# Gate and up projections of a gated feed-forward layer: seven block products in place of eight, with the weight factors kept in DRAM

## What is computed

```python
def ffn(x, w_gate, w_up, w_down):
    h = silu(x @ w_gate) * (x @ w_up)
    h_sparse = _sparsify_2to4(h)      # of each 4 neighbours the 2 with the largest |h|
    return h_sparse @ w_down
x = x + tanh(g_xattn[0]) * cross_attention(layernorm(x), ctx, mask)
x = x + tanh(g_ffn[0]) * ffn(layernorm(x), w_gate, w_up, w_down)
```

## Time and profile before

| | |
|---|---|
| median of 3 runs | 1212.21 us (1211.08 to 1212.95) |
| the profiled execution, from first to last instruction (span) | 1210.4 us |
| PE busy | 1189.7 us, 98% |
| DVE busy | 755.0 us, 62% |
| ACT busy | 428.7 us, 35% |
| POOL busy | 103.4 us, 9% |
| DMA | 80.48 MB, 66 GB/s over the span; 235 to 320 GB/s in the attention phase |

### The profile page before, as it was taken

The page is one execution under the profiler, slowest core; times in us unless marked ns, Lnnn a source line. Parts: engine busy times, 40 slices in busy tenths (PEclk is TensorE's granted clock), DMA queues, the critical chain, the costliest instruction groups (busy, mean ns, idle before and its releaser), DMA issues.

```text
span 1210.4 us, 15963 instructions
## 1 busy us (share of the span) xinstructions
PE 1189.7 (98%) x5344; PEld 954.2 (79%) x5344; DVE 755.0 (62%) x1289; ACT 428.7 (35%) x788; POOL 103.4 (9%) x281
## 2 busy tenths in 40 slices
PE   7998989999999999999999999999999999999998
PEld 6776768888888888888888888888888888888887
DVE  7999465556667555556667555555667655555565
ACT  6889432222225233222234322322244332232221
POOL 6777410000000000000000000000000000000000
PEclk9999889999999999999999999999999999999999
DMA  6886220000001030010101030001101001111101
GB/s 238 264 240 189 95 105 35 35 35 35 35 35 70 1 131 8 35 35 35 35 35 69 0 139 31 4 35 35 35 35 69 35 1 69 69 69 69 69 35 70
DMA packets 40245, 80.48 MB, mean 66 GB/s; under 512 B 2720, under 2 KB 19104, under 8 KB 35616
## 3 DMA queue, kind: packets, MB, share of 16 engines
q1 hardware_dynamic: 40224, 80.23, 19.1%
HBM read 63.44 MB, written 16.78 MB: 66 GB/s over the span
## 4 chain that ended last, share of the span: by engine, by line
PE 88%; DVE 1%; ACT 0%; issue 0%; ACTq 0%; DVEq 0%
PE ps_y L62 10%; PE ps_y L63 10%; PE ps_y L64 10%; PE ps_up L62 10%; PE ps_gate L62 10%; PE ps_up L63 10%; PE ps_up L64 10%; PE ps_gate L63 10%; PE ps_gate L64 10%; DVE beats L735 0%; ACT h_hi L722 0%; DVE part L769 0%; DVE part L770 0%; DVE rows L742 0%; DVE hidden L781 0%; DVE wins L773 0%
## 5 line engine op out<-in xcount | busy, mean ns | idle before, releaser
L753 DVE TENSOR_TENSOR hidden<-ps_up,silu 128x512 f32<-128x512 f32 x128 | 88.4, 691 | 412.2 <-PE ps_up L64 411.0
L702 ACT ACTIVATE hidden_abs<-hidden 128x512 f32<-128x512 f32 x128 | 81.0, 633 | 375.0 <-DVE hidden L753 375.0
L62 PE MATMUL ps_gate<-x_hi,gu_hi 128*128 128x512 f32 x496 | 196.9, 397 | 3.3 <-ACT silu L700 3.3
L63 PE MATMUL ps_gate<-x_lo,gu_hi 128*128 128x512 f32 x496 | 197.0, 397 | 0.0
L64 PE MATMUL ps_gate<-x_hi,gu_lo 128*128 128x512 f32 x496 | 196.9, 397 | 0.0
L62 PE MATMUL ps_y<-dn_hi,h_hi 128*128 128x512 f32 x496 | 196.3, 396 | 0.0
L63 PE MATMUL ps_y<-dn_lo,h_hi 128*128 128x512 f32 x496 | 196.2, 396 | 0.0
L64 PE MATMUL ps_y<-dn_hi,h_lo 128*128 128x512 f32 x496 | 196.2, 396 | 0.0
L62 PE MATMUL ps_up<-x_hi,gu_hi 128*128 128x512 f32 x496 | 196.2, 395 | 0.0
L63 PE MATMUL ps_up<-x_lo,gu_hi 128*128 128x512 f32 x496 | 196.1, 395 | 0.0
L64 PE MATMUL ps_up<-x_hi,gu_lo 128*128 128x512 f32 x496 | 195.9, 395 | 0.0
(11 more groups left out here) (88 smaller groups left out, 1325.3 us busy)
## 6 DMA issues: line engine op xcount, KB each, us to landing
x_raw<-xnT_scratch SPq DMA_DIRECT2D x32, 1024.0 KB, 4.8
x_in<-in_x SPq DMA_DIRECT2D x32, 256.0 KB, 3.0
ctx_in<-in_ctx SPq DMA_DIRECT2D x32, 256.0 KB, 3.1
xnT_scratch<-x1nT SPq DMA_DIRECT2D x32, 256.0 KB, 2.8
out_rows<-rows SPq DMA_DIRECT2D x7, 1024.0 KB, 5.0
gu_raw<-in_L_ffn_w_gate SPq DMA_DIRECT2D x4, 1024.0 KB, 5.1
gu_raw<-in_L_ffn_w_up SPq DMA_DIRECT2D x4, 1024.0 KB, 7.3
gu_raw<-in_L_ffn_w_down SPq DMA_DIRECT2D x4, 1024.0 KB, 6.6
```

Source lines behind the costliest of these rows:

```text
L62: nc.tensor.matmul(bank, a_hi, b_hi, start=start, stop=False)
L63: nc.tensor.matmul(bank, a_hi, b_lo, start=False, stop=False)
L702: nc.scalar.activation(hidden_abs[:, j], hidden[:, j], ACT.Abs).then_inc(abs_done, 1)
L753: nc.vector.tensor_tensor(hidden[:, j], ps_up[j % 2][:], silu[:, j % 2], ALU.mult).then_inc(hidden_done, 1)
```

## The change

The gate and up products of one feature pair (2 groups j) and 1024 rows are taken as one two by two block product. On the weight side the blocks are gate and up, each in two halves of the contraction; on the row side they are the two halves of the contraction and two halves of 512 rows. Sums and differences of blocks on either side give seven factors each, and seven products (k = 0 to 6), each for the two features e of the pair, replace eight. Such a piece of work is a **unit**; there are 32, two to a **step** s (unit 2s the even one, 2s+1 the odd one). A unit has 7 x 2 x 6 = 84 matmuls, then 48 of the down product of an earlier step: half of the rows in the even unit, the other half in the odd one. Units 0 and 1 have no down product, and two down products stand alone at the end.

The products accumulate in PSUM. Bank `ps_a` holds product 0, is copied to SBUF by ACT (`copy_a0`), takes product 2 on top, is copied again (`copy_a1`), takes product 4 and is read by DVE (`add_c22`), and takes product 6. `ps_d` takes 3 (`copy_d0`) and 5, `ps_c` takes 1. DVE adds the copies to the banks (`add_c11`, `add_c22`, `add_c12`). PE waits for `a0_copied` before product 2, `a1_copied` before 4, `d0_copied` before 5, `c22_done` before 6, and for `y_added` of two tiles back at each tile of the down product, which now has two PSUM banks (`ps_y`) where it had four.

The weight factors differ for each of the 8 (quarter, feature pair) units. They are built while units 0 to 6 run, each for the unit after it (`BUILT` = 8; unit 0's in the attention phase): four raw pieces of 512 KB come one after the other through one buffer (`w_raw`), ACT spreads each (`spread`), DVE makes four sums (`w_sum`), ACT and DVE split seven factors (`w_high`, `w_low`), and SP stores them (512 KB each) to `w_scratch`. Units 8 to 31 load them from there, 3.67 MB a unit. The row factors of 1024 rows (a pair of blocks, `xm`) are built one or more at each of five points of a step for the next pair, and go through `xm_scratch`; the first pair's are built in the attention phase, with POOL taking the low parts of them and of unit 0's weights (`W0_AT`, `X0_AT`). The x1 rows no longer stay in SBUF: `rows` holds 8 sequences, the other 24 go to `x1_scratch` in the attention phase and come back a pair at a time. The loops are written out in full in the program.

Core of the diff (parts left out are the attention stages, which keep their order, the loops' unrolling, and declarations):

```diff
-                for c in range(KC):
-                    last = three_products(nc, ps_up[j % 2][:], gu_hi[:, 1, j, c], gu_lo[:, 1, j, c],
-                                          b_hi[:, c], b_lo[:, c], c == 0, c == KC - 1)
-                last.then_inc(up_done, 1)
...
+                if k == 2:
+                    pe.wait_ge(a0_copied[e], u + 1)
+                if k == 3:
+                    wait(pe, c12_done[e], u)
+                    if u == 0:
+                        pe.wait_ge((pT_copied, nT_copied)[e], B)
+                if k == 4:
+                    pe.wait_ge(a1_copied[e], u + 1)
+                if k == 5:
+                    pe.wait_ge(d0_copied[e], u + 1)
+                if k == 6:
+                    pe.wait_ge(c22_done[e], u + 1)
+                to = bank[k][e][:]
+                begins = k in (0, 1, 3)
+                for c in range(2):
+                    nc.tensor.matmul(to, w_ring[:, k, e, 0, c], xm[:, k, 0, c], start=begins and c == 0, stop=False,
+                                     skip_group_check=not begins)
+                    nc.tensor.matmul(to, w_ring[:, k, e, 0, c], xm[:, k, 1, c], start=False, stop=False,
+                                     skip_group_check=not begins)
+                    last = nc.tensor.matmul(to, w_ring[:, k, e, 1, c], xm[:, k, 0, c], start=False, stop=c == 1,
+                                            skip_group_check=not begins)
+                last.then_inc(made[k], 1)
...
+        def load_w_piece(sp, u, blk):
+            wait(sp, spread_done, 4 * u + blk)
+            view = (gate_view, up_view)[blk // 2]
+            q = u // 2
+            sp.dma_start(w_raw[:], view[:, 2 * (blk % 2):2 * (blk % 2) + 2, q * IQ:(q + 1) * IQ]
+                         ).then_inc(w_raw_loaded, 16)
...
+        def spread(act, u, blk):
+            act.wait_ge(w_raw_loaded, 16 * (4 * u + blk + 1))
+            wait(act, w_lo_done, 7 * u)
+            g = u % 2
+            nc.scalar.activation(w_blk[:, blk], w_raw[:].rearrange("p c (m j) -> p j c m", j=GROUP)[:, 2 * g:2 * g + 2],
+                                 ACT.Copy).then_inc(spread_done, 1)
+        def w_high(act, u, k):
+            if k in (0, 1, 6):
+                act.wait_ge(spread_done, 4 * u + (1, 2, 0, 0, 0, 0, 4)[k])
+            else:
+                act.wait_ge(sums_done, 4 * u + (0, 0, 3, 1, 2, 4)[k])
+            if u > 0:
+                act.wait_ge(made[k], 2 * u)
+                act.wait_ge(w_stored[k], 16 * u)
+            nc.scalar.activation(w_ring[:, k, :, 0], w_blk[:, W_FROM[k]], ACT.Copy).then_inc(w_hi_done, 1)
+        def w_low(engine, instructions, u, k):
+            engine.wait_ge(w_hi_done, 7 * u + k + 1)
+            instructions.tensor_tensor(w_ring[:, k, :, 1], w_blk[:, W_FROM[k]], w_ring[:, k, :, 0].bitcast(F32),
+                                       ALU.subtract).then_inc(w_lo_done, 1)
...
+        def x_low(engine, instructions, p, k, i):
+            high, low = x_to(p, k, i)
+            engine.wait_ge(x_hi_done, 7 * (2 * p + k) + i + 1)
+            instructions.tensor_tensor(low, x_blk[:, X_FROM[i]], high.bitcast(F32), ALU.subtract).then_inc(x_lo_done, 1)
...
+                if n in W0_AT:
+                    w_low(pool, nc.gpsimd, 0, W0_AT[n])
+                if n in X0_AT:
+                    x_low(pool, nc.gpsimd, 0, *X0_AT[n])
+            for q in range(QS):
+                for j in range(GROUP):
+                    pool.wait_ge(dn_hi_done, GROUP * q + j + 1)
+                    nc.gpsimd.tensor_tensor(dn[:, 1, j], dn[:, 1, j].bitcast(F32), dn[:, 0, j].bitcast(F32),
+                                            ALU.subtract).then_inc(dn_lo_done, 1)
...
+                building = u + 1 < BUILT
+                if s > 0:
+                    absolute(s - 1, 1, 0)
+                copy_a0(u, 0)
+                if s > 0:
+                    absolute(s - 1, 1, 1)
+                copy_a0(u, 1)
+                if s > 0:
+                    h_high(s - 1, 0, 0)
+                    h_high(s - 1, 0, 1)
+                    absolute(s - 1, 1, 2)
+                    absolute(s - 1, 1, 3)
+                    h_high(s - 1, 0, 2)
+                    h_high(s - 1, 0, 3)
+                if 0 < s <= QS:
+                    for j in range(GROUP):
+                        dn_high(s - 1, j)
+                silu0(u, 0)
+                silu0(u, 1)
+                if building and s > 0:
+                    spread(act, u + 1, 0)
+                copy_a1(u, 0)
+                if building and s > 0:
+                    spread(act, u + 1, 1)
+                copy_a1(u, 1)
+                copy_d0(u, 0)
+                if building and s > 0:
+                    spread(act, u + 1, 2)
+                copy_d0(u, 1)
+                if building and s > 0:
+                    spread(act, u + 1, 3)
+                if building:
+                    w_high(act, u + 1, 0)
+                    w_high(act, u + 1, 1)
+                if s > 0:
+                    for j in range(GROUP):
+                        h_high(s - 1, 1, j)
+                silu1(u, 0)
+                silu1(u, 1)
+                if building:
+                    for k in range(2, PROD):
+                        w_high(act, u + 1, k)
...
+            for s in range(STEPS):
+                u = 2 * s
+                building = u + 1 < BUILT
+                if s > 0:
+                    keep(s - 1, 0)
+                add_c11(u, 0)
+                add_c11(u, 1)
+                if s > 0:
+                    for j in range(GROUP):
+                        h_low(s - 1, 0, j)
+                    compare(s - 1, 1, FIRST + REST)
+                add_c22(u, 0)
+                add_c22(u, 1)
+                if s > 0:
+                    count_wins(s - 1, 1)
+                add_c12(u, 0)
+                add_c12(u, 1)
+                if s > 0:
+                    keep(s - 1, 1)
+                    for j in range(GROUP):
+                        h_low(s - 1, 1, j)
+                gated0(u, 0)
+                gated1(u, 0)
+                gated0(u, 1)
+                gated1(u, 1)
+                if building and s > 0:
+                    w_sum(dve, u + 1, 0)
+                    w_sum(dve, u + 1, 1)
+                if s > 0:
+                    add_y(s - 1, 0, 0)
+                if building:
+                    w_low(dve, nc.vector, u + 1, 0)
+                    w_sum(dve, u + 1, 2)
+                    w_low(dve, nc.vector, u + 1, 1)
+                    w_sum(dve, u + 1, 3)
+                if s > 0:
+                    add_y(s - 1, 0, 1)
+                if building:
+                    w_low(dve, nc.vector, u + 1, 2)
+                    w_low(dve, nc.vector, u + 1, 3)
+                if s > 0:
+                    add_y(s - 1, 0, 2)
+                if building:
+                    w_low(dve, nc.vector, u + 1, 4)
+                    w_low(dve, nc.vector, u + 1, 5)
+                    w_low(dve, nc.vector, u + 1, 6)
+                if s > 0:
+                    add_y(s - 1, 0, 3)
+                x_low_at(s, 0)
...
+                for t in range(TILES):
+                    n = TILES * hs + t
+                    wait(pe, y_added, n - 1)
+                    if n < 2:
+                        pe.wait_ge(x1_done, B)
+                    at = slice(t * P, (t + 1) * P)
+                    to = ps_y[n % 2][:]
+                    for j in range(GROUP):
+                        if t == 0:
+                            pe.wait_ge(h_lo_done, GROUP * hs + j + 1)
+                        nc.tensor.matmul(to, h_hi[:, h, j, at], dn[:, 0, j], start=j == 0, stop=False)
+                        nc.tensor.matmul(to, h_hi[:, h, j, at], dn[:, 1, j], start=False, stop=False)
+                        last = nc.tensor.matmul(to, h_lo[:, h, j, at], dn[:, 0, j], start=False, stop=j == GROUP - 1)
+                    last.then_inc(y_done, 1)
+            for u in range(UNITS):
+                for k in range(PROD):
+                    for e in range(2):
+                        product(u, k, e)
+                if u >= 2:
+                    down(u // 2 - 1, u % 2)
+            down(STEPS - 1, 0)
```

```diff
+            for s in range(STEPS):
+                p = s // QS
+                u = 2 * s + 1
+                if u < BUILT:
+                    if s > 0:
+                        for blk in range(1, 4):
+                            load_w_piece(sp, u, blk)
+                        if u + 1 < BUILT:
+                            load_w_piece(sp, u + 1, 0)
+                    for k in range(PROD):
+                        store_w(u, k)
+                else:
...
+                x_stored_at(s, 0)
+                u = 2 * s + 2
+                if u < BUILT:
+                    x_stored_at(s, 1)
+                    for blk in range(1, 4):
+                        load_w_piece(sp, u, blk)
+                    load_w_piece(sp, u + 1, 0)
+                    x_stored_at(s, 2)
```

(11 more changed lines are left out.)

1240 lines of the change are left out of this document (663 added, 577 removed).

## The result

The changed kernel takes 1347.9 us (median of 4 runs, 1345.6 to 1348.6) against 1212.6 us (4 runs, 1211.1 to 1213.1): a ratio of 1.1116, 95% interval 1.1100 to 1.1131. It is slower, as forecast, but by 135 us instead of 38, and outside the range. The span of the profiled execution is 1345.9 us.

A forecast was written before the change was run, and what follows sets the result against it. PE was taken to bound the feed-forward phase and DVE the attention phase. 150 (attention) + 985.5 (4224 matmuls) + 85 (building) + 17 (steady waits) + 10 (tail) + 3.2 (end) = 1250.7 us span; forecast 1250, range 1185 to 1290.

The forecast's parts named there:

- Attention phase: Attention phase: POOL's low parts and the spreads lengthen its slots, so it ends near 150 us instead of 125.7.
- A slot becomes 3.28 + 1.55 - 0.39: Attention slots: one POOL low part, less idle time, makes a slot 4.44 us; 21 x 1.16 = 24 us.
- DMA ends last: Rival, chance 0.12: attention stretches to 160 us and raw pieces queue behind stores; 1295 us in all.
- Building: Units that build weights: copies stand behind spreads waiting for raw pieces, and DVE ends late; 85 us with clock.
- four times POOL's `dn_low` [...] and the clock [...]: some 10: Building units: POOL's low parts of down weights holding DVE, and 2.7 us of slow clock per long wait; some 10 us.
- The rival with 0.14: All matmuls: the faster pace, 1.36 us for six, holds; 28 us less, 1222 us, still slower; chance 0.14.
- What sets it the trace doesn't tell: Matmul pace: the trace leaves open what sets 1.36 or 1.40 us for six; the operands' tiles differ.
- Steady waits: Steps 4 to 15: PE's third down-product tile waits 1.3 us in the even unit; 12 x 1.4 = 17 us.
- Clock in steady steps: Rival, chance 0.05: each 1.3 us wait of steps 4 to 15 costs 2.7 us of clock; 32 more, 1282.
- Tail: After the last unit: DVE's work delays the first add_y, so the two down products end 10 us later.
- The sign: Whole kernel: slower than before, 1250 us against 1212.6; chance of slower 0.68, faster 0.28, same 0.04.
- the building is hidden: Rival, chance 0.28: building work fits ahead of need, so the kernel is faster; 1178 us with all low bounds.

The follow-up runs named there:

- e1: Changed kernel with POOL taking each low part of the attention phase one slot after ACT makes its high part: 1314.3 us span against 1345.9.
- e2: Changed kernel with the attention phase's eight spreads two slots apart, each piece loaded a slot before its spread: 1331.6 us span against 1345.9.
- e3: Changed kernel with both attention edits, POOL's low parts a slot later and the spreads two slots apart: 1301.8 us span against 1345.9.
- e12: e3 with DVE in place of POOL taking the 21 low parts of the attention phase: 1302.4 us span against 1301.8.
- e10: Changed kernel without building in the feed-forward phase (unit 0's factors everywhere), with e1, e2, e9 and later row factors: 1180.2 us span against 1345.9.
- e9: Changed kernel with the even unit's first add_y ahead of the four gated products on DVE: 1329.9 us span against 1345.9.
- e5: Changed kernel without building or storing weight factors in the feed-forward phase, unit 0's factors used everywhere: 1252.0 us span against 1345.9.
- e16: A reordered version of the changed kernel (1259.9 us span) with row factors moved behind first spread, silu1 and products, rows stored later: 1285.0 us span.

## Why the prediction was wrong

The sum again, as predicted and as the trace has it:

| term | predicted | measured |
|---|---|---|
| start of the feed-forward phase | 150 | 209.6, and 5.0 for the first copy |
| 4224 matmuls | 985.5 | 960.0 (0.2273 each) |
| waits and clock in units 0 to 7 | 85 | 114.5 (332.7 less 960 x 0.2273) |
| units 8, 9 and 17 | 0 | 23.8 (10.0 + 7.0 + 6.8 over 30.0) |
| waits of steady steps | 17 | 18.9 |
| tail and end | 13.2 | 13.9 |
| span | 1250.7 | 1345.7 |

**Attention phase, the step that failed most (+64.6).** "A slot becomes 3.28 + 1.55 - 0.39": that took POOL's occupancy as the price. But POOL's low part waits for ACT's high part, which stands behind ACT's xn, which waits for POOL's small instructions; the price was the way round, 2.5 us a slot and more, where the sum had 1.16. e1 shows it by starting the same instruction on finished data: then it costs 1.1 to 1.6 us, about the price in the sum. A duration of 1.27 us instead of 1.55 made it no cheaper. The eight spreads were given 0.5 each; with their pieces loaded only a slot ahead ACT waited 31.7 us, most of it in the two slots of 20.9 and 14.7 us, and e2 gave back 14.3. The "DMA ends last" rival expected a long phase too (160), and in the stretch from 60 to 70 us the DMA share is indeed 0.85 at 301 GB/s; but with the same bytes the phase became 45 us shorter by order alone (e3). So the DMA did not set this phase; it may set what is left. Some 45 us over before remain in the best version, about half of them in the late start and the three long slots named under e3; the rest I haven't separated. DVE lost next to nothing beside POOL, where the prediction reckoned with up to 22 us: in e3, from 30 to 160 us, its 14 sums of two blocks in SBUF took 2 us more together than in e12, where POOL has no low parts, and all its other instructions took the same.

**Building (+29.5 in units 0 to 7).** Place, order and releasers were as predicted: PE waits for L590, ACT for `w_raw`, 4.8 us from spread to spread. Units 3 and 5 took 47.0 and 41.7 (predicted 37.0), units 4 and 6 took 51.8 and 51.1 (46.0). Units 1 and 2 were shared out wrongly: 44.5 and 46.2, where the prediction has some 25 and 57. The down weights were there 14.7 us into unit 4, not at 12 at best; SP's issues in a row of stores took 0.8 us each, for which the prediction had nothing. The whole stretch, units 0 to 7:

```profile
209.60:542.20 332.60, 251.39 (x941) 196.82 (x940) 195.62 (x317) 140.80 (x233) 15.27 (x12) 0.84 0.56 207
```

PE is idle for 81 us, close to the 75 of the prediction's waits (19 of its 960 matmuls are missing from the trace, so up to 4 us of that may be work). It is busy for 251 us, where 960 matmuls at 0.2273 need 218: some 33 us went to the lower clock, granted at 0.84 in the mean. The sum had 2.7 us for each of a few waits. So "four times POOL's `dn_low` [...] and the clock [...]: some 10" was the mis-sized term.

**Units 8, 9 and 17 (+23.8) had no term.** Unit 8 builds nothing but splits the last down weights; units 9 and 17 store and reload the rows of a pair on SP, behind which the row factor's store waits, and ACT's copies behind that factor. In unit 9 ACT stands 6.3 us for that store, while the DMA engines are busy for 0.98 of the time:

```profile
597.00:602.00 5.00, 1.48 (x8) 0.93 (x6) 0.69 (x1) 1.57 (x4) 0.00 (x0) 1.00 0.98 366
```

**Pace (-25.5).** The rival with 0.14 was right: it said 28 us less, and it was 25.5. It hides as much of the errors above. "What sets it the trace doesn't tell" still stands. The kernel before ran its matmuls 0.2328 apart (859 in 200 us), every version of the new one 0.2273. The kernel before has both: its own first step runs at 0.227 (131.1 to 147.6 us), and from the first matmul of the next step (147.86) to the end it is 0.233, whichever bank is written. In e10 from 800 to 1000 us, with PE busy throughout as before:

```profile
800.00:1000.00 200.00, 200.00 (x882) 165.28 (x881) 140.62 (x229) 70.36 (x123) 0.00 (x0) 1.00 0.60 222
```

**Steady waits: right** in place, size (1.35 us, 1.3 predicted) and mechanism, which e9 shows; an even unit lost 1.8 us in all. **Clock in steady steps: no.** The row of 600 to 800 us above has three such waits and a clock of 0.99, and from 858 to 1290 us PE waits eight times for `rows` L860 (10.8 us) while full clock is granted throughout. The Trainium skill, TensorE: Matmul & The Clock Gate, section on a second failure mode, has PE's brief idling between groups make the clock go back and forth; by that rule these steps would have cost 32 us more, and here the trace disagrees. **Tail: right in size, wrong in cause.** DVE was to hold it; the last 2 MB of down weights did, since their load waits for the product before:

```profile
1309.93 0.32 SPq L353 DMA_DIRECT2D dn<-dn_scratch  x1
...
1317.97 0.80 PE L1077 MATMUL ps_y<-dn,h_hi 128*128 128x512 f32 x1 [8.06 <-DMA dn<-dn_scratch]
```

**The sign** held because the gain, 384 matmuls, was 89.6 us (115 with the pace), and two costs of that size stood against it: the phase began 84 us after before's attention phase ended (209.6 against 125.7), and the building cost 92 us (e5). The low bounds of "the building is hidden" gave 1178, and only the version that leaves the building out comes there (e10, 1180). The order can be mended to 1236, and what then remains of the building is 46 us in units 1 to 6.

## What to carry to other kernels

An instruction given to a spare engine is priced by the ring that it closes, not by its length: follow its input back and its successor forward until the same engine comes again, and if it does, start it one iteration late. Fewer matmuls move the load to everything that feeds and empties them: count for every moved unit of work what stands behind it on its engine, and price a one-buffer stream as load plus use, in turns. Before reordering by hand, leave the whole added work out once (e10 here): it says what the best order can be worth. And where waits come one after another, price the slower clock beside the waits themselves: here it cost 33 us beside 81 us of idle time.

## What the runs showed of the hardware that was not expected

The pace of matmuls of 128x512 was 0.2273 us in the new kernel and 0.2328 in the old one at the same granted clock of 1.00, with the same three-product pattern; the old one changes from 0.227 to 0.233 at the start of its second step, and what sets it no run tells. POOL's subtraction of 128x512 took 1.27 us where before showed 1.55 and 1.73. An issue on SP took 0.32 us alone (1309.93) and 0.82 in a row of stores (five in 4.12 us at 374.41).

DVE beside POOL: in e16, while POOL takes four low parts of `dn` (from about 472.7 to 479.3 us), these stand on DVE:

```profile
459.89 2.49 DVE L852 TENSOR_TENSOR h_lo<-hidden,h_hi 128x512 fp32r<-128x512 f32 x4
...
472.44 2.36 DVE L845 SCALAR_TENSOR_TENSOR hidden<-beats,hidden 128x512 f32<-128x512 bf16 x2
...
476.40 4.62 DVE L852 TENSOR_TENSOR h_lo<-hidden,h_hi 128x512 fp32r<-128x512 f32 x4
```

The same four splits take 2.49 us without POOL and 4.62 beside it; POOL's four take 6.38 us here, and 4.96 in the after kernel. The Trainium skill, SBUF — State Buffer, section Who interferes with whom, says that a VectorE instruction with two SBUF inputs contends with GpSimd; all of these have two, and the trace agrees. In the attention phase it came to 2 us (e3 against e12, above).
